# An expert pass whose silu product is transposed by VectorE, with wide weight pieces, an early silu, and projections whose key pass has no transposes

## What is computed

```python
x = x + _L0_xattn_ref(_layernorm(x), ctx_2048, mask, Wq, bq, Wk, bk, Wv, bv, Wo, bo, ...)
x = x + _L0_ffn_ref(_layernorm(x), gate_weight, w_gate, w_up, w_down)
# _L0_ffn_ref: logits = x @ gate_weight.T; the top 8 of softmax, made to sum to 1; then for each expert
g = ragged_dot(sorted_tokens, w_gate, group_sizes)
u = ragged_dot(sorted_tokens, w_up, group_sizes)
out = ragged_dot(silu(g) * u, w_down, group_sizes)      # weighted and added up for each token
```

## Time and profile before

| what | value |
|---|---|
| median of 3 runs | 6708.36 us (6706.5 to 6711.54) |
| profiled execution, its own time | 6714.65 us |
| its span from first to last instruction | 6713.0 us |
| TensorE busy | 6472.6 us (96%) |
| VectorE busy | 3663.3 us (55%) |
| ScalarE busy | 2923.7 us (44%) |
| GpSimd busy | 2308.0 us (34%) |
| granted TensorE clock, mean | 0.983 |

### The profile page before, as it was taken

The page is one execution under the profiler, slowest core; times in us unless marked ns, Lnnn a source line. Parts: engine busy times, 40 slices in busy tenths (PEclk is TensorE's granted clock), DMA queues, the critical chain, the costliest instruction groups (busy, mean ns, idle before and its releaser), DMA issues.

```text
span 6713.0 us, 107844 instructions
## 1 busy us (share of the span) xinstructions
PE 6472.6 (96%) x32234; PEld 5731.1 (85%) x32235; DVE 3663.3 (55%) x4544; ACT 2923.7 (44%) x3606; POOL 2308.0 (34%) x2178
## 2 busy tenths in 40 slices
PE   9999999999999999699999999999999999999998
PEld 7888887887888788589989888899899999989987
DVE  4443324999999799744454454443533444444444
ACT  3321224888888655333343343332422333333333
POOL 1000000000000155544545454554444444545554
PEclk9999999999999999899999999999999999999999
DMA  8863555555555676456676676665655656666666
GB/s 258 232 196 143 155 146 144 127 128 127 128 132 130 174 173 171 110 152 160 163 212 162 164 188 160 163 164 111 186 111 111 139 137 164 146 155 164 161 158 149
DMA packets 873577, 1049.72 MB, mean 156 GB/s; under 512 B 440705, under 2 KB 670849, under 8 KB 873474
## 3 DMA queue, kind: packets, MB, share of 16 engines
q0 software_dynamic: 123984, 368.70, 24.0%
q1 hardware_dynamic: 593104, 382.50, 23.6%
q10 hardware_dynamic: 156386, 297.29, 13.2%
HBM read 725.85 MB, written 322.31 MB: 156 GB/s over the span
## 4 chain that ended last, share of the span: by engine, by line
PE 33%; DMA 8%; issue 6%; DVE 4%; POOL 3%; ACT 2%; ACTq 1%; SPq 0%; another core or an unknown queue 0%; POOLq 0%; DVEq 0%
DMA out<-moe_y,moe_rec_s 4%; PE moe_ps_gate L1374 4%; PE moe_ps_gate L1375 4%; PE moe_ps_gate L1376 4%; PE moe_ps_up L1376 4%; PE moe_ps_up L1374 4%; PE moe_ps_up L1375 4%; PE moe_ps_y L1363 3%; PE moe_ps_y L1362 3%; PE moe_ps_y L1361 3%; DMA moe_tokens<-h2st,moe_rows 3%; POOL moe_tokens L1325 2%; DVE moe_ps_turned L1477 1%; DVE moe_d_lo L1467 1%; DVE moe_gu_lo L1467 1%
## 5 line engine op out<-in xcount | busy, mean ns | idle before, releaser
L1325 POOL DMA_INDIRECT moe_tokens<-h2st,moe_rows x1156 | 1273.1, 1101 | 515.2 <-issue 265.7
L1374 PE MATMUL moe_ps_gate<-moe_gu_hi,moe_xT_hi 128*128 128x384 f32 x2288 | 811.3, 355 | 73.8 <-DVE moe_xT_lo L1471 53.9
L1414 ACT COPY moe_y<-moe_ps_y 128x1024 f32<-128x1024 f32 x287 | 291.2, 1015 | 1249.4 <-DMA out<-moe_y,moe_rec_s 1051.9
L1375 PE MATMUL moe_ps_gate<-moe_gu_lo,moe_xT_hi 128*128 128x384 f32 x2288 | 784.4, 343 | 0.0
L1376 PE MATMUL moe_ps_gate<-moe_gu_hi,moe_xT_lo 128*128 128x384 f32 x2288 | 783.4, 342 | 0.0
L1376 PE MATMUL moe_ps_up<-moe_gu_hi,moe_xT_lo 128*128 128x384 f32 x2288 | 764.3, 334 | 0.0
L1375 PE MATMUL moe_ps_up<-moe_gu_lo,moe_xT_hi 128*128 128x384 f32 x2288 | 764.2, 334 | 0.0
L1374 PE MATMUL moe_ps_up<-moe_gu_hi,moe_xT_hi 128*128 128x384 f32 x2288 | 764.2, 334 | 0.0
L1484 DVE SCALAR_TENSOR_TENSOR moe_hidden<-moe_silu,moe_rec_w,moe_ps_up 128x384 f32<-128x384 f32 x286 | 175.8, 615 | 1009.2 <-PE moe_ps_up L1376 694.4
L1361 PE MATMUL moe_ps_y<-moe_d_hi,moe_hT_hi 128*128 128x512 f32 x1722 | 673.5, 391 | 12.8 <-DVE moe_hT_lo L1491 10.3
L1363 PE MATMUL moe_ps_y<-moe_d_hi,moe_hT_lo 128*128 128x512 f32 x1722 | 677.1, 393 | 0.0
(11 more groups left out here) (202 smaller groups left out, 14047.6 us busy)
## 6 DMA issues: line engine op xcount, KB each, us to landing
first_raw<-in_w_gate ACTq DMA_DIRECT2D x63, 1536.0 KB, 7.7
first_raw<-in_w_up ACTq DMA_DIRECT2D x63, 1536.0 KB
moe_raw_d<-in_w_down ACTq DMA_DIRECT2D x63, 1536.0 KB
proj_a_raw<-in_ctxT POOLq DMA_DIRECT2D x64, 512.0 KB, 5.6
kst<-proj_o SPq DMA_DIRECT2D x256, 128.0 KB, 2.8
vst<-proj_o SPq DMA_DIRECT2D x64, 512.0 KB, 2.6
qst<-proj_o SPq DMA_DIRECT2D x256, 128.0 KB, 2.2
att_kt<-kst SPq DMA_DIRECT2D x64, 512.0 KB, 3.5
```

Source lines behind the costliest of these rows:

```text
L1325: nc.gpsimd.indirect_dma_start(out=tokens[:, g * (H // G):(g + 1) * (H // G)], out_offset=None, in_=h2_quarters, in_offset=bass.IndirectOf ...
L1374: nc.tensor.matmul(o[:, 0:I], xT_hi[:, c], gu_hi[:, b, k, c], start=(c == 0), stop=False)
L1375: nc.tensor.matmul(o[:, 0:I], xT_hi[:, c], gu_lo[:, b, k, c], start=False, stop=False)
```

## The change

In the projections TensorE no longer transposes in the key pass. The normalized rows are stored to DRAM as they are (`xnst`, with their columns in another order), the query pass loads them in groups of 32 rows, and VectorE turns each quarter of a block with one block transpose of 128x1024 (`turn`, 32 in all).

In the expert pass:

- the gate and up weights are split in 4 pieces of 128x1536 in place of 8 of 128x768, and on VectorE they stand between the other steps of the first tile;
- TensorE's three transposes of `hidden` are gone. VectorE makes the same 128x384 transpose by 16 instructions (`turn_hidden`), each of which takes 32 partitions by 3 times 32 columns and writes them to another group of 32 partitions in PSUM;
- ScalarE's silu of tile t+1 stands at the end of tile t's list (`gated`), so at an expert's end it comes ahead of the three down pieces; `load_down` moved from the list's end into the next expert's first tile;
- the row numbers for the gathers are computed by VectorE (`token_rows`), no longer by GpSimd, right behind `turn_tokens`.

The diff, cut to its core (line numbers of the changed kernel differ by a few):

```diff
@@ projections_pass
-        acc, tps = s.ps("acc", [P, BANKS, HALF]), s.ps("tps", [P, 2, C, P])
+        rows = s.sb("rows", [P, 4, H])
+        xin, xn = rows[:, 0:2], rows[:, 2:4]
+        xg = rows[:].rearrange("p q n -> p (q n)").rearrange("p (g n) -> p g n", g=GROUPS)
+        acc = s.ps("acc", [P, BANKS, HALF])
...
 (load, on GpSimd's queue)
+                    if p == Q:
+                        if not is_first(t2, b):
+                            pool.wait_ge(turned_done, PIECES * t)
+                        for k in range(P // W):
+                            part = xnst[bass.ds(t * HALF, HALF), k * (H * W // P):(k + 1) * (H * W // P)]
+                            pool.dma_start(xg[k * W:(k + 1) * W], part.rearrange("(g b) n -> b g n", b=W)).then_inc(xg_in, 16)
+                        return
...
 (body, SyncE)
-                            sp.dma_start(xnT_v[:, :, bass.ds(j * P, P)], xT[:, jb]).then_inc(xT_stored[jb], 16)
+                            sp.dma_start(xnst[bass.ds(j * P, P), :], xn[:, jb]).then_inc(xn_stored[jb], 16)
...
 (VectorE, called for the query pass ahead of evacuate)
+                def turn(p, t2, b, k):
+                    n = number(p, t2, b)
+                    dve.wait_ge(xg_in, 16 * (P // W) * (2 * t2 + b + 1))
+                    dve.wait_ge(a_lo_done, (n - 1) * PIECES + k + 1)
+                    columns_of_piece = slice(k * CP * W, (k + 1) * CP * W)
+                    nc.vector.transpose(a_raw[:, chunks(k)].rearrange("p c t -> p (c t)"), xg[:, :, columns_of_piece]).then_inc(turned_done, 1)
...
 (TensorE, key pass)
-                            for c in range(C):
-                                last = nc.tensor.transpose(tps[:, jb, c], xn[:, jb, c * P:(c + 1) * P], ident[:])
-                            last.then_inc(t_done, 1)
@@ experts_pass
+        CHUNKS = C // 2
+        GU = 2 * C // CHUNKS
+        PIECES = GU + CI
...
-                for c in range(0, C, 2):
-                    yield raw[:, c:c + 2], raw_in[k], gu_hi[:, b, k, c:c + 2], gu_lo[:, b, k, c:c + 2]
+                for c in range(0, C, CHUNKS):
+                    yield raw[:, c:c + CHUNKS], raw_in[k], gu_hi[:, b, k, c:c + CHUNKS], gu_lo[:, b, k, c:c + CHUNKS]
...
 (gather, GpSimd)
-                    nc.gpsimd.tensor_scalar(rows[:], rec_g[:].bitcast(I32)[:, :, 0], float(G), group[:], ALU.mult, ALU.add).then_inc(rows_done, 1)
...
 (tile, TensorE)
                     down(t - 1, b_before)
-                    pe.wait_ge(hidden_done, t + 2)
-                    for c in range(CI):
-                        last = nc.tensor.transpose(hT_ps[:, c], hidden[:, c * P:(c + 1) * P], ident[:])
-                    last.then_inc(hT_done, 1)
...
 (ScalarE)
-                def tile(t, e=None, b=None, more=False, is_first=False):
-
+                def gated(t):
                     act.wait_ge(gu_done, 2 * t + 1)
                     act.wait_ge(hidden_done, t + 1)
                     nc.scalar.activation(silu[:], gate_ps[:, 0:I], ACT.Silu).then_inc(silu_done, 1)
-                    tokens_high(t + 1)
-                    if e is not None:
-                        split(e, b, 0, GU)
-                    output(t - 1, is_first)
+
+                def turned_high(t):
                     act.wait_ge(hT_done, t + 2)
                     nc.scalar.copy(hT_hi[:], hT_ps).then_inc(hT_hi_done, 1)
+
+                def tile(t):
+                    tokens_high(t + 1)
+                    output(t - 1)
+                    turned_high(t)
+                    gated(t + 1)
+
+                def first_tile(t, e, b, more, is_first):
+                    tokens_high(t + 1)
+                    load_down(e)
+                    split(e, b, 0, 2)
+                    output(t - 1, is_first)
+                    split(e, b, 2, 3)
+                    turned_high(t)
+                    split(e, b, 3, GU)
+                    gated(t + 1)
                     if more:
-                        load_gate_up(e + 1)
+                        load_gate_up(e + 1, 0)
+                        load_gate_up(e + 1, 1)
...
                         split(e + 1, 1 - b, GU, PIECES)
-                        if has_second:
-                            load_down(e + 2)
...
 (VectorE)
+                def token_rows(t):
+                    dve.wait_ge(rec_g_in, 16 * G * (t + 1))
+                    if not (isinstance(t, int) and t == 0):
+                        dve.wait_ge(gathered, 16 * G * t)
+                    nc.vector.tensor_scalar(rows[:], rec_g[:].bitcast(I32)[:, :, 0], float(G), group[:], ALU.mult, ALU.add).then_inc(rows_done, 1)
...
+                def turn_hidden(t):
+                    dve.wait_ge(hidden_done, t + 2)
+                    dve.wait_ge(hT_lo_done, t + 1)
+                    columns = hidden[:].rearrange("p (j q) -> p j q", q=P)
+                    for g in range(G):
+                        for k in range(G):
+                            rows_g, rows_k = slice(g * W, (g + 1) * W), slice(k * W, (k + 1) * W)
+                            last = nc.vector.transpose(hT_ps[rows_k, :, rows_g], columns[rows_g, :, rows_k])
+                    last.then_inc(hT_done, 1)
...
                     tokens_low(t + 1)
+                    if e is not None:
+                        split(e, b, 0, 1)
                     turn_tokens(t + 2)
+                    token_rows(t + 3)
                     if e is not None:
-                        split(e, b, 0, GU)
+                        split(e, b, 1, 2)
+                    turn_hidden(t)
+                    if e is not None:
+                        split(e, b, 2, 3)
                     dve.wait_ge(hT_hi_done, t + 1)
                     nc.vector.tensor_tensor(hT_lo[:], hT_ps, f32(hT_hi[:]), ALU.subtract).then_inc(hT_lo_done, 1)
+                    if e is not None:
+                        split(e, b, 3, GU)
```

163 lines of the change are left out of this document (72 added, 91 removed).

## The result

The changed kernel takes 6817.9 us (median of 4 runs, 6809.4 to 6819.7) against 6709.4 us: ratio 1.0159, 95% interval 1.0143 to 1.0175. It is slower by 108 us, where 76 were forecast. The profiled execution took 6819.70 us.

The account below looks back on a forecast made before the run. TensorE was taken to bound the kernel by its issue, waits and clock. The terms -28 - 97 - 153 + 240 + 80 + 4 + 30 = +76 on 6708 gave 6785 us, range 6560 to 6900.

Parts of the forecast that it names:

- What bounds it: Whole kernel: TensorE, busy 96% of the span, sets the time by what it issues, its few waits and its clock.
- Key pass, -28: Key pass: without TensorE's eight transposes each of 32 tiles saves 0.89 us, 28 us in all.
- Transposes off TensorE, -97: Expert tiles: without TensorE's three transposes of hidden each of 285 tiles saves 0.34 us, 97 us in all.
- VectorE's chain: An expert's first tile, timed from its first gate matmul (s): VectorE's list ends hT_lo at 24.65, stalling the next down product 3.8 us.
- The price of a transpose, 0.32: VectorE's sixteen block transposes of hidden: 0.32 us each without overlap, since each changes its partition group; 5.1 us a tile.
- rival A: VectorE's sixteen transposes overlap at 0.21 us each, hT_lo is 2.1 late, time about 6575 us; chance 0.32.
- Stalls, +240 + 4 + 30: TensorE's stalls: 240 us for hT_lo behind 63 first tiles, 4 for late xT_lo, 30 in six single-tile experts.
- The clock, +80: Behind the hT_lo stalls: half of 63 bring a fall to half clock, 2.5 us each, 80 us in all.
- Rival B: TensorE's clock falls behind every stall, 3.4 us each, 214 us in place of 80, time about 6920 us; chance 0.10.
- The early silu, -153: Expert stage: silu ahead of the down-weight casts removes all loss except start-up and weight waits, clock losses included: 153 us.
- Row numbers at nothing: Row numbers moved from GpSimd to VectorE: no cost or gain counted, as GpSimd's slack hides either place.
- The sum: Whole kernel: all terms add up to +76 us, giving 6785 us.

Follow-up runs that it names:

- e12: Kernel before with the early silu (down-weight load moved into the first tile) and the changed kernel's projections: 6631 us, 0.9893 of the kernel before.
- e6: Kernel before with the early silu alone, the load of the down weights moved into the first tile: 6667 us, 0.9945 of the kernel before.
- e4: Changed kernel with the projections of before put back (TensorE transposes in the key pass, no block transposes in the query pass): 6868 us, 1.0229 of the kernel before.
- e3: Changed kernel with each of the sixteen transposes writing the 32-partition group it reads, so the result is another matrix: 6685 us, 0.9957 of the kernel before.
- e1: Changed kernel with TensorE's three transposes of hidden back and VectorE's sixteen gone: 6683 us, 0.9950 of the kernel before.
- e5: Changed kernel with the transposes of hidden back on TensorE and the row numbers back on GpSimd: 6738 us, 1.0046 of the kernel before.
- e8: Changed kernel with TensorE transposing hidden in first tiles only, VectorE in the others, and row numbers on GpSimd: 6853 us, 1.0222 of the kernel before.
- e7: Changed kernel with only the row numbers back on GpSimd: 6803 us, 1.0152 of the kernel before.

## Why the prediction held, step by step

- **What bounds it, right.** TensorE's beat plus its waits plus its clock give the time: 285 x 12.47 = 3554 us of beat in 3957.8 of the stage.
- **Key pass, -28: right.** The stage began 29.2 us earlier; e12 against e6 gives 35 (each ratio is known to some 11 us), e4 30.6 up to the first tile.
- **Transposes off TensorE, -97: right.** 285 x 0.31 = 88 us by the two plain tiles.
- **VectorE's chain, right in size by two errors.** `hidden` was put at s + 10.6, `hT_lo` at its end at 24.65, 3.8 late. Measured: `hidden` at 6126.95, s + 11.8, `hT_lo` at s + 25.3. The table reads that I took at 1.0 cost 0.41 at most (6126.54 to 6126.95), so they were too dear; but the casts began later: the timeline of ScalarE has the silu at s + 6.4, not 4.5, with 1.33 us of waiting that the profile puts to no engine, and the low halves begin at s + 7.9, not 6.1:

```profile
6119.77 0.48 ACT L1421 CAST moe_hT_hi<-moe_ps_hT 128x384 fp32r<-128x384 f32 x1 [3.29 <-issue]
...
6121.58 0.49 ACT L1417 ACTIVATE moe_silu<-moe_ps_gate 128x384 f32<-128x384 f32 x1 [1.33 <-remote]
...
6121.97 2.93 ACT L1388 CAST moe_d_hi<-moe_raw_d 128x1024 fp32r<-128x1024 f32 x3
...
6124.81 1.01 ACT L1394 CAST moe_xT_hi<-moe_ps_turned 128x1024 fp32r<-128x1024 f32 x1
```

  So the next tile started 0.94 late and the down product 3.21 later: 4.15 in place of 0.06 + 3.8.
- **The price of a transpose, 0.32: right,** measured 0.302. The reason, no overlap because the group changes, was tested by e3 and held in its main part: 0.195 where it changes only every fourth time. But the prediction took the change to be between what an instruction reads and what it writes; four of the sixteen make no such change and are as slow, and what counts is the change from one output to the next. By that fifteen of the sixteen are held and not all: the first starts at 6133.43, 0.08 before the piece ahead of it ends. And the four memsets, which it counted for rival A as without a pause, speak against it when their starts are read: in the trace of before they are 0.06 us long and 0.11 apart.
- **Stalls, +240 + 4 + 30: right in sum.** 179.0 us for `hT_lo`, 38.1 for `xT_lo`, 37.5 for weight pieces: 255. The term of 4 was mis-sized (38.1), the one of 240 covers 179.
- **The clock, +80: about right, its sharing out not.** The mean clock over the span fell from 0.983 to 0.972. At half clock that is 2 x 0.028 x 6818 less 2 x 0.017 x 6713 = some 150 us more of time at 1.2 GHz, which lose at most half. Of what the terms of beat, key pass and waits leave open, 105 + 29 + 88 - 151 = 71 us (151: the waits' 260 with all rows of the list, less the 109 of before without the start-up), the clock can be all. The tiles show where: those behind a first tile lose 288 us and stand for 174 of them, which leaves 114 where I had put 80, while of the old losses beside standing (75 us before) some 35 are left in the other tiles. In the 60 matmuls behind a stall at the down product the distances added up to 0.7 us over those of a plain tile in 7 cases without a fall, to 1.7 in 34 with a fall of 3.4 us and to 2.8 in 15 with one of 6.8: falls are more frequent than the half that I took, and cheaper than 2.5. Rival B had the frequency nearly right and the price (3.4) too high.
- **The early silu, -153: the term that stands worst.** Inside the changed kernel TensorE's waits for `hidden` are gone, and tiles between and last ones run at the beat; but the first tiles still lose 81 us of their 89, now by waits for `xT_lo` (38.1, where 4 were forecast), for weight pieces and by clock. And e6, which makes this edit alone, gained 37: behind the silu stands the next chain, the tokens' transpose, gather, scatter, copy of y and `hT_hi`, which in the changed kernel has 3 us more time in each expert's second tile since TensorE stands there. That this standing is what pays for it, is an inference from e1, e5, e6 and e8, which all lose in later tiles when the stall is gone; no run lengthened a stall by itself.
- **Row numbers at nothing: right here, wrong as a rule.** e7 against the changed kernel nothing, e5 against e1 64 us; in e7 they meet one wide piece and take 1.56 us, in e5 mostly two and 3.14.
- **The sum.** +76 against +105 in the profiled executions. As loss over the beat in the stage the prediction left 181 - 153 + 240 + 80 + 4 + 30 = 382 us, and 404 were measured. Its price for the tile behind a first one, 3.8 + 0.5 x 2.5 = 5.05 us, 288 in 57, is to the microsecond what came, and that is partly luck: the standing was 3.1 and the clock's share 2.0. The forecast's mechanism is shown by e1 (the transposes' move alone costs 140 us net) and by e3 (their distance alone decides the sign). What the early silu is worth in the changed kernel is argued only.
